# Turning activations through VectorE and a DRAM trip instead of TensorE, in a fused feed-forward, attention, feed-forward kernel

## The chip, the cores and the metric

One core of one Trainium2 chip runs the kernel. The metric is the device time of one execution in microseconds. Three runs of the kernel before give a median of 175.92 us (175.82 to 176.13). "TensorE" (PE in the rows) multiplies, "VectorE" is DVE, "ScalarE" is ACT, "GpSimd" is POOL, and SP is the queue that issues most transfers.

## What is computed

Three residual blocks over x of 4 x 1024 tokens of 128 numbers, in f32:

```
x = x + 0.5 * ffn(layernorm(x))      # first
x = x + attention(layernorm(x))      # linear attention, 16 heads of 8
x = x + 0.5 * ffn(layernorm(x))      # second, same weights

ffn(x):  lt = x[:, 1:17]; even = lt[:, ::2]; odd = lt[:, 1::2]
         m1 = outer(even[:4], odd[:4]) as (512, 128); m2 = outer(even[4:], odd[4:]) as (128, 512)
         h = gelu(x @ (W1 + scale * m1).T + b1);  out = h @ (W2 + scale * m2).T + b2
attn(x): q, k, v = x @ W.T + b;  f(t) = exp(t @ R - 0.5 * |t|^2), t scaled by 1/sqrt(8)
         out = (f(q) @ (f(k).T @ v)) / sum(f(q));  out @ Wo.T + bo
```

W1 and W2 differ for each batch row of x, since `m1` and `m2` come from its own first tokens.

## The kernel before

**Tiles.** Tokens go in chunks of 512 (4 tiles of 128 tokens). There are 16 feed-forward chunks: 0 to 7 in the first part, 8 to 15 in the second, two for each batch row; attention has its own 8. All of x stays in SBUF, in the tile `X`, in three generations.

**A feed-forward chunk f.** VectorE takes statistics (`stats`, L112) and aggregates them (`moments`, L120, L124), GpSimd takes the power -1/2 (L342), VectorE makes the offset (`norm`), ScalarE writes the normalized tile `xn` (L399), tokens on the partitions. The product with W1 needs features on the partitions. Stage `turn` does that: four TensorE transposes of 128x128 into the PSUM bank `ps_t` (L677), ScalarE copies the bank to `xh`, rounded to the short form fp32r (L410), and VectorE subtracts `ps_t - xh` into `xl` (L527). Stage `up.f.j` is three matmuls of 128x512, `xh*w1h + xl*w1h + xh*w1l` (L712 to L714), and a Gelu on ScalarE (L432). Stage `down.f.n` is eight records of 128x128 in f32 (L728); after the fourth, VectorE adds into `X` (L595).

**Weights of a batch row.** `rows.i` sends 16 token rows to DRAM and fetches them back to all partitions as `ev` (L297, L304). `odd` takes the odd tokens from the turned chunk (L535), `w1` adds to W1 (L557), ScalarE rounds (`w1h`), VectorE takes the rest (`w1l`, L568), `w2` adds to W2 (L581). For batch row 0, `w1.0` on VectorE makes all four blocks, rounding included (L562, L564), from rows that TensorE picks out (`select`).

**Attention.** `astats`, `anorm` and `aturn` do for attention's input what `stats`, `norm` and `turn` do: four transposes into `ps_m` (L700), `xah` on ScalarE (L413), `xal` on VectorE (L539). `qk` is three matmuls for each token tile (L745 to L747) into a pair of PSUM banks; `feat` squares on ScalarE (L438), `head_sums` adds per head on VectorE (L604), `feat` subtracts there (L611), `exp` on ScalarE (L446) writes `qk`. Then come `gram` (L763), `z_sums`, `z_eps`, `z` (L617 to L625, and GpSimd's L374), `qturn` (L752), `mix` (L775, L778; VectorE copies its result to `mo`, L635) and `o` (L785, added at L640).

**What sets the order.** Each engine runs its instructions in program order, and the order of stages is written out by hand in the table `ORDER`, one list for each engine. Semaphores carry the dependences. SP works through its list in order as well, and a wait in it holds all that stands behind.

A turn before, on three engines:

```
ins = pe.transpose(ps_t[:, n * P:(n + 1) * P], xn[:, i % XN, n], ident[:])
act.activation(xh[:, i % XT], ps_t[:], ACT.Copy).then_inc(s_hi, 1)
dve.tensor_tensor(xl[:, i % XT], ps_t[:], xh[:, i % XT].bitcast(F32), ALU.subtract)
```

Of the kernel before, what the change touches and what calls it, by code (L numbers as in the profile page):

```python
# [820 lines left out]
```

## Time and profile before

| | us |
|---|---|
| median of three runs | 175.92 |
| the profiled execution's own time | 174.35 |
| its span, first to last instruction | 172.6 |
| TensorE busy | 166.8 |
| VectorE busy | 127.4 |
| ScalarE busy | 123.2 |
| GpSimd busy | 69.4 |

The span is shorter than the execution's time by what lies around the first and last instruction. TensorE's end times are modelled, so its busy time says that it had work in hand, not that it ran at its peak. A group of instructions ("L677 PE MATMUL ...") gives busy time and the mean duration of one; on VectorE and ScalarE an instruction begins before the one ahead of it has fully ended, so the distance between two starts is what one costs.

### The profile page before, as it was taken

What the parts mean: (1) busy time and instruction counts of PE and PEld (TensorE: products, weight loads), DVE (VectorE), ACT (ScalarE), POOL (GpSimd) and SP (SyncE); (2) the same over time, 40 slices, a digit from 0 to 9 for tenths busy, and PEclk for the clock granted to TensorE, in tenths of its full rate; (3) what the DMA queues carried; (4) which work ended last, traced back from release to release, by engine and by line L of the source; (5) the groups of instructions that cost most, each with busy time, mean ns of one, the idle gap of its engine ahead of it and who ended that gap; (6) DMA issues with size and microseconds to landing.
All of it is one profiled execution on the core that took longest, in us unless ns stands there. A gap on an engine that the chain in (4) does not pass through costs nothing.

```text
span 172.6 us, 3454 instructions
## 1 busy us (share of the span) xinstructions
PE 166.8 (97%) x1132; PEld 148.8 (86%) x1132; DVE 127.4 (74%) x446; ACT 123.2 (71%) x241; POOL 69.4 (40%) x85
## 2 busy tenths in 40 slices
PE   6999999999999999999999999899999999999993
PEld 6976998898899989768788898789899989898893
DVE  1888798977967647899999999998957664651111
ACT  3498669598796958779955499986894757557500
POOL 4522196232188089862522544004451399200000
PEclk9999999999999999999999999999999999999999
DMA  4993100404000000000000004310005003521203
GB/s 107 291 281 100 50 0 3 124 4 122 2 0 4 0 2 4 0 0 0 0 0 6 0 4 122 91 36 2 4 8 176 0 0 88 161 90 32 66 13 108
DMA packets 17009, 9.06 MB, mean 53 GB/s; under 512 B 1008, under 2 KB 16608, under 8 KB 16992
## 3 DMA queue, kind: packets, MB, share of 16 engines
q1 hardware_dynamic: 16704, 8.85, 17.4%
q8 instruction: 9, 0.15, 0.4%
q14 instruction: 8, 0.07, 0.1%
q10 hardware_dynamic: 288, 0.00, 0.1%
HBM read 6.69 MB, written 2.15 MB: 51 GB/s over the span
## 4 chain that ended last, share of the span: by engine, by line
PE 90%; DVE 5%; issue 2%; ACT 1%; POOL 0%; POOLq 0%; DVEq 0%; ACTq 0%
PE quad L728 32%; PE quad L712 9%; PE quad L713 9%; PE quad L714 9%; PE ps_t L677 4%; PE quad L745 4%; PE quad L663 4%; PE quad L747 3%; PE quad L746 3%; PE ps_g L763 3%; PE ps_m L700 2%; PE ps_t L785 2%; PE ps_r L752 1%; DVE s L604 1%; PE ps_g L728 1%
## 5 line engine op out<-in xcount | busy, mean ns | idle before, releaser
L728 PEld LDWEIGHTS quad<-w2e,gl 128*128 128x128 f32 x496 | 59.9, 192 | 2.4 <-ACT gl L432 0.2
L728 PE MATMUL quad<-w2e,gl 128*128 128x128 f32 x496 | 60.7, 275 | 0.0
L432 ACT ACTIVATE gl<-quad,cols 128x512 f32<-128x512 f32 x64 | 43.5, 686 | 20.6 <-PE quad L714 20.3
L712 PE MATMUL quad<-xh,w1h 128*128 128x512 f32 x64 | 28.7, 448 | 0.6 <-DVE w1l L568 0.2
L342 POOL TENSOR_TENSOR rstd<-veps,mhalf 128x4 f32<-128x4 f32 (+1 forms) x16 | 16.1, 1011 | 31.3 <-DVE veps L124 29.5
L399 ACT ACTIVATE xn<-X,nmr,rstd 128x128 f32<-128x128 f32 x61 | 24.8, 484 | 3.6 <-DVE nmr L499 3.6
L713 PE MATMUL quad<-xl,w1h 128*128 128x512 f32 x64 | 25.3, 395 | 0.0
L714 PE MATMUL quad<-xh,w1l 128*128 128x512 f32 x64 | 25.2, 394 | 0.0
L595 DVE TENSOR_TENSOR X<-quad,X 128x512 f32<-128x512 f32 (+1 forms) x16 | 10.8, 673 | 15.6 <-PE quad L728 9.9
L363 POOL TENSOR_TENSOR X<-X,b2h 128x512 f32<-128x512 f32 x16 | 20.6, 1311 | 4.1 <-issue 4.1
L374 POOL TENSOR_TENSOR qn<-qk,zr 128x512 f32<-128x512 f32 x8 | 8.6, 1081 | 23.7 <-DVE zr L625 23.6
L112 DVE BATCH_NORM_STATS2 bst<-X 128x6 f32<-128x128 f32 x64 | 13.7, 278 | 4.3 <-DMA X<-in_x_dram 4.2
L712 PEld LDWEIGHTS quad<-xh,w1h 128*128 128x128 f32 x64 | 12.2, 190 | 3.8 <-DVE w1l L564 1.3
L438 ACT ACTIVATE sq<-quad 128x512 f32<-128x512 f32 x16 | 9.5, 595 | 8.1 <-PE quad L747 7.7
L527 DVE TENSOR_TENSOR xl<-ps_t,xh 128x512 fp32r<-128x512 f32 x16 | 10.9, 684 | 5.5 <-ACT xh L410 5.2
L745 PE MATMUL quad<-wah,xah 128*128 128x512 f32 x32 | 14.3, 447 | 0.5 <-DVE ex L611 0.3
L714 PEld LDWEIGHTS quad<-xh,w1l 128*128 128x128 f32 x64 | 12.0, 188 | 2.8
L348 POOL TENSOR_TENSOR arstd<-aveps,mhalf 128x4 f32<-128x4 f32 x8 | 8.1, 1011 | 15.8 <-DVE aveps L124 15.8
L581 DVE SCALAR_TENSOR_TENSOR w2e<-ev,od,w2t 128x128 f32<-128x128 f32 x28 | 11.5, 477 | 3.3 <-DMA ev<-token_rows 3.3
L422 ACT ACTIVATE xa<-X,anmr,arstd 128x128 f32<-128x128 f32 x32 | 13.0, 483 | 0.0
L713 PEld LDWEIGHTS quad<-xl,w1h 128*128 128x128 f32 x64 | 12.2, 191 | 0.8
L747 PE MATMUL quad<-wah,xal 128*128 128x512 f32 x32 | 12.6, 395 | 0.0
(108 smaller groups left out, 279.7 us busy)
## 6 DMA issues: line engine op xcount, KB each, us to landing
ev<-token_rows SPq DMA_DIRECT2D x7, 512.0 KB, 3.7
X<-in_x_dram SPq DMA_DIRECT2D x7, 256.0 KB, 6.4
out_dram<-X SPq DMA_DIRECT2D x7, 256.0 KB, 2.9
w1t<-in_w1t_dram SPq DMA_DIRECT2D x1, 256.0 KB, 3.6
w2n<-in_w2t_dram SPq DMA_DIRECT2D x1, 256.0 KB, 4.7
wa<-in_wa_dram SPq DMA_DIRECT2D x1, 256.0 KB, 6.7
out_dram<-X SPq DMA_DIRECT2D x2, 128.0 KB, 1.8
X<-in_x_dram SPq DMA_DIRECT2D x1, 192.0 KB, 3.3
```

The lines of the kernel that those rows point to most:

```text
L112: ins = dve.bn_stats(bst[:, i, n], x[:, n])
L342: pool.tensor_tensor(rstd[:, i, own], veps[:, i, own], mhalf[:, own], ALU.pow).then_inc(s_rstd, 1)
L363: pool.tensor_tensor(X[:, after], X[:, before], b2h[:].unsqueeze(1).to_broadcast([P, NT, D]), ALU.add).then_inc(s_xb, 1)
L399: act.activation(xn[:, i % XN, n], X[:, xslot(i), n], ACT.Identity, bias=nmr[:, i, n:n + 1], scale=rstd[:, i, n:n + 1]).then_inc(s_xn, 1)
L422: act.activation(xa[:, i, n], X[:, CHUNKS + i, n], ACT.Identity, bias=anmr[:, i, n:n + 1], scale=arstd[:, i, n:n + 1]).then_inc(a_xn, 1)
L432: act.activation(gl[:, f % 2, j], ps_h[j % 2], ACT.Gelu, bias=cols[:, j:j + 1]).then_inc(s_gelu, 1)
L712: pe.matmul(ps_h[j % 2], w1h[:, w, blk], xh[:, f % XT], start=True, stop=False)
L713: pe.matmul(ps_h[j % 2], w1h[:, w, blk], xl[:, f % XT], start=False, stop=False)
L714: pe.matmul(ps_h[j % 2], w1l[:, w, blk], xh[:, f % XT], start=False, stop=True).then_inc(s_u, 1)
L728: ins = pe.matmul(y[:, n * P:(n + 1) * P], gl[:, f % 2, j, n * P:(n + 1) * P], w2e[:, f // PER_B % 2, j], start=(j == 0), stop=(j == HB - 1))
L745: pe.matmul(to, xah[:, a, tile], wah[:], start=True, stop=False)
L747: pe.matmul(to, xal[:, a, tile], wah[:], start=False, stop=True).then_inc(s_qk, 1)
```

## The change

Only chunks 0 to 3 are still turned by TensorE. Chunks 4 to 15 and all eight inputs of attention go another way:

- VectorE's block transpose (`blocks`, `ablocks`) turns each 32x32 block of the normalized chunk in place of its partition quadrant, and writes them to `tq` or `atq` (two slots each) in an order that suits the store.
- SP writes 256 KB to the new DRAM tensor `folded` (`put`, `aput`), waits until it has landed, and reads it back with four transfers of 32 partitions (`land`, `aland`) into `land` (three slots) or `aland` (two).
- ScalarE and the subtraction then read `land` or `aland` in SBUF instead of PSUM. For attention the subtraction goes to GpSimd; `xah` and `xal` shrink from eight slots to five.
- `z_eps` goes from VectorE to GpSimd, the copy to `mo` from VectorE to ScalarE, the rounding of the first W1 blocks from VectorE to ScalarE in four stages `first_w1h`, between VectorE's `first_w1` and `first_w1l`.
- x chunk 3 is loaded before W2, chunks 4 to 7 before `wa` and `rrep`; `w2n` goes, `w2t` is scaled in place. `ps_o` is `ps_t` for all chunks. `ORDER` is new on all five lists.

```diff
+PE_TURNS = (0, 1, 2, 3)
+BY_DRAM = [f for f in range(FC) if f not in PE_TURNS]
+SQ = 32
+LAND, ALAND, TQ, AH = 3, 2, 2, 5
...
+        def folding(t):
+            return t.rearrange("p (b n i) -> p n b i", n=NT, i=SQ)
+        def in_order(t):
+            return t.rearrange("p (q n i) -> p n q i", n=NT, i=SQ)
+        def turned(f):
+            return as_tiles(ps_t[:]) if f in PE_TURNS else in_order(land[:, by_dram(f) % LAND])
+        def as_tiles(t):
+            return t.rearrange("p (n q i) -> p n q i", n=NT, i=SQ)
...
+                if stage == "put":
+                    sp.wait_ge(s_tr, by_dram(i) + 1)
+                    sp.dma_start(folded[i], tq[:, by_dram(i) % TQ]).then_inc(s_put[i], 16)
+                if stage == "land":
+                    sp.wait_ge(s_put[i], 16)
+                    if by_dram(i) >= LAND:
+                        gone = BY_DRAM[by_dram(i) - LAND]
+                        sp.wait_ge(s_lo, gone + 1)
+                        sp.wait_ge(s_od, gone // PER_B + 1)
+                    for b in range(D // SQ):
+                        place = slice(SQ * b, SQ * (b + 1))
+                        sp.dma_start(land[place, by_dram(i) % LAND].rearrange("p (q c) -> p q c", q=P // SQ),
+                                     folded[i].rearrange("(q p) (b c) -> b p q c", p=SQ, c=P)[b]).then_inc(s_land[i], 16)
...
+                if stage == "aturn":
+                    pool.wait_ge(a_hi, i + 1)
+                    pool.tensor_tensor(as_tiles(xal[:, i % AH]), in_order(aland[:, i % ALAND]),
+                                       as_tiles(xah[:, i % AH].bitcast(F32)), ALU.subtract).then_inc(a_lo, 1)
...
-                    act.wait_ge(s_xt, i + 1)
+                    if i in PE_TURNS:
+                        act.wait_ge(s_xt, by_pe(i + 1))
+                    else:
+                        act.wait_ge(s_land[i], 16 * D // SQ)
                     wait(act, s_u, HB * (i - XT + 1))
-                    act.activation(xh[:, i % XT], ps_t[:], ACT.Copy).then_inc(s_hi, 1)
+                    act.activation(as_tiles(xh[:, i % XT]), turned(i), ACT.Copy).then_inc(s_hi, 1)
...
-                    dve.tensor_tensor(xl[:, i % XT], ps_t[:], xh[:, i % XT].bitcast(F32), ALU.subtract).then_inc(s_lo, 1)
+                    dve.tensor_tensor(as_tiles(xl[:, i % XT]), turned(i), as_tiles(xh[:, i % XT].bitcast(F32)),
+                                      ALU.subtract).then_inc(s_lo, 1)
...
+                if stage == "blocks":
+                    dve.wait_ge(s_xn, normed(i, NT - 1))
+                    k = by_dram(i)
+                    if k >= TQ:
+                        dve.wait_ge(s_put[BY_DRAM[k - TQ]], 16)
+                    dve.transpose(folding(tq[:, k % TQ]), as_tiles(flat(xn[:, i % XN]))).then_inc(s_tr, 1)
...
-                if stage == "aturn":
-                    wait(pe, a_lo, i)
...
-                    for n in range(NT):
-                        pe.wait_ge(a_xn, NT * i + n + 1)
-                        ins = pe.transpose(ps_m[:, n * P:(n + 1) * P], xa[:, i, n], ident[:])
-                    ins.then_inc(a_xt, 1)
```

The order at three places. TensorE in attention, around the second chunk's "qk" (`xah` is attention's turned input), before:

```order
L728 MATMUL quad<-w2e,gl 128x128 x8
L700 MATMUL ps_m<-ident,xa 128x128 x4
L728 MATMUL quad<-w2e,gl 128x128 x12
L745 MATMUL quad<-wah,xah 128x512
L746 MATMUL quad<-wal,xah 128x512
L747 MATMUL quad<-wah,xal 128x512
L745 MATMUL quad<-wah,xah 128x512
L746 MATMUL quad<-wal,xah 128x512
L747 MATMUL quad<-wah,xal 128x512
L700 MATMUL ps_m<-ident,xa 128x128 x4
```

and changed:

```order
L822 MATMUL quad<-wal,xah 128x512
L823 MATMUL quad<-wah,xal 128x512
L821 MATMUL quad<-wah,xah 128x512
L822 MATMUL quad<-wal,xah 128x512
L823 MATMUL quad<-wah,xal 128x512
L821 MATMUL quad<-wah,xah 128x512
L822 MATMUL quad<-wal,xah 128x512
L823 MATMUL quad<-wah,xal 128x512
L821 MATMUL quad<-wah,xah 128x512
L822 MATMUL quad<-wal,xah 128x512
```

The transposes `ps_m<-ident,xa` between the "qk" matmuls are gone. VectorE in the middle of attention, before:

```order
L539 TENSOR_TENSOR xal<-ps_m,xah 128x512
L604 TENSOR_REDUCE s<-sq 128x64
L621 TENSOR_SCALAR zs<-zs 128x64
L611 TENSOR_TENSOR ex<-quad,s 128x512
L625 RECIPROCAL zr<-zs 128x64
L604 TENSOR_REDUCE s<-sq 128x64
L539 TENSOR_TENSOR xal<-ps_m,xah 128x512
L611 TENSOR_TENSOR ex<-quad,s 128x512
L617 TENSOR_REDUCE zs<-qk 128x64
L604 TENSOR_REDUCE s<-sq 128x64
L539 TENSOR_TENSOR xal<-ps_m,xah 128x512
```

and changed:

```order
L699 TENSOR_REDUCE s<-sq 128x64
L712 TENSOR_REDUCE zs<-qk 128x64
L706 TENSOR_TENSOR ex<-quad,s 128x512
L626 STREAM_TRANSPOSE atq<-xa 128x4x4x32
L699 TENSOR_REDUCE s<-sq 128x64
L716 RECIPROCAL zr<-zs 128x64
L706 TENSOR_TENSOR ex<-quad,s 128x512
L699 TENSOR_REDUCE s<-sq 128x64
L712 TENSOR_REDUCE zs<-qk 128x64
L706 TENSOR_TENSOR ex<-quad,s 128x512
L626 STREAM_TRANSPOSE atq<-xa 128x4x4x32
```

`xal` and `z_eps` (the TENSOR_SCALAR on `zs`) no longer stand there; `atq<-xa`, a block transpose, does. SP in the second feed-forward part, before:

```order
L304 DMA ev<-token_rows 128x8x128
L297 DMA token_rows<-xn 16x128
L304 DMA ev<-token_rows 128x8x128
L312 DMA out_dram<-X 128x4x128
L297 DMA token_rows<-xn 16x128
L304 DMA ev<-token_rows 128x8x128
L312 DMA out_dram<-X 128x4x128 x6
```

and changed (`folded<-tq` is a put, `land<-folded` a landing in four transfers):

```order
L351 DMA folded<-tq 128x512
L361 DMA land<-folded 32x4x128 x4
L351 DMA folded<-tq 128x512
L361 DMA land<-folded 32x4x128 x4
L351 DMA folded<-tq 128x512
L341 DMA token_rows<-xn 16x128
L348 DMA ev<-token_rows 128x8x128
L351 DMA folded<-tq 128x512
L361 DMA land<-folded 32x4x128 x4
L351 DMA folded<-tq 128x512
L361 DMA land<-folded 32x4x128 x8
L341 DMA token_rows<-xn 16x128
```

Puts and landings now stand between the `rows` steps, and later output stores wait behind them.

## Rows read from the trace of the kernel before

**Rows 1.** The page, part 1: busy time, share of the span, instructions of each engine.
```profile
span 172.6 us, 3454 instructions
...
PE 166.8 (97%) x1132; PEld 148.8 (86%) x1132; DVE 127.4 (74%) x446; ACT 123.2 (71%) x241; POOL 69.4 (40%) x85
```

**Rows 2.** The page, part 2: clock granted to TensorE, 40 slices, tenths of full speed.
```profile
PEclk9999999999999999999999999999999999999999
```

**Rows 3.** The page, part 4: the chain that ended last, by line.
```profile
PE quad L728 32%; PE quad L712 9%; PE quad L713 9%; PE quad L714 9%; PE ps_t L677 4%; PE quad L745 4%; PE quad L663 4%; PE quad L747 3%; PE quad L746 3%; PE ps_g L763 3%; PE ps_m L700 2%; PE ps_t L785 2%; PE ps_r L752 1%; DVE s L604 1%; PE ps_g L728 1%
```

**Rows 4.** The chain in order of time: start us, length us, what.
```profile
11.50 0.48 PE quad L712
...
17.90 1.78 PE quad L728 x16
...
23.93 0.44 PE ps_t L677 x4
...
63.66 0.23 PE quad L745
...
111.09 0.47 PE quad L712
```

**Rows 5.** The same chain where it leaves TensorE, 101 to 110 us; one piece of many.
```profile
103.64 0.86 DVE bst L112 x4
```

**Rows 6.** Stretches: length, busy of PE, PEld, DVE, ACT, POOL, PEclk, DMA share, GB/s.
```profile
65.72:110.14 44.42, 43.59 (x284) 37.32 (x283) 43.32 (x122) 35.72 (x75) 21.56 (x23) 1.00 0.05 13
111.00:170.00 59.00, 58.83 (x420) 53.98 (x420) 33.90 (x113) 37.42 (x68) 17.53 (x15) 1.00 0.21 61
```

**Rows 7.** The timeline of VectorE: start us, us, engine, line, operation, output<-input.
```profile
41.72 1.49 DVE L581 SCALAR_TENSOR_TENSOR w2e<-ev,od,w2t 128x128 f32<-128x128 f32 x4
...
67.04 0.87 DVE L112 BATCH_NORM_STATS2 abst<-X 128x6 f32<-128x128 f32 x4
67.94 0.69 DVE L539 TENSOR_TENSOR xal<-ps_m,xah 128x512 fp32r<-128x512 f32 x1
68.55 0.37 DVE L120 BATCH_NORM_AGGREGATE amv<-abst 128x2 f32<-128x6 f32 x4
...
69.03 0.68 DVE L611 TENSOR_TENSOR ex<-quad,s 128x512 f32<-128x512 f32 x1
...
77.46 0.18 DVE L621 TENSOR_SCALAR zs<-zs 128x64 f32<-128x64 f32 x1
...
107.62 0.28 DVE L635 COPY mo<-ps_m 128x128 f32<-128x128 f32 x1
...
109.46 0.68 DVE L527 TENSOR_TENSOR xl<-ps_t,xh 128x512 fp32r<-128x512 f32 x1
```

**Rows 8.** VectorE and GpSimd side by side; then all passes of w1l (min/median/max ns).
```profile
52.83 2.52 POOL L363 TENSOR_TENSOR X<-X,b2h 128x512 f32<-128x512 f32 x2
...
54.12 2.48 DVE L581 SCALAR_TENSOR_TENSOR w2e<-ev,od,w2t 128x128 f32<-128x128 f32 x4
...
L568 DVE TENSOR_TENSOR w1l<-w1r,w1h x7: 691/693/1174, 21.7 to 152.4; 128x512 fp32r<-128x512 f32 x7
```

**Rows 9.** Groups of instructions, GpSimd: passes over 512 elements.
```profile
L363 POOL TENSOR_TENSOR X<-X,b2h 128x512 f32<-128x512 f32 x16 | 20.6, 1311 | 4.1 <-issue 4.1
...
L374 POOL TENSOR_TENSOR qn<-qk,zr 128x512 f32<-128x512 f32 x8 | 8.6, 1081 | 23.7 <-DVE zr L625 23.6
```

**Rows 10.** DMA issues, KB, us to landing; and the timeline of SP.
```profile
ev<-token_rows SPq DMA_DIRECT2D x7, 512.0 KB, 3.7
X<-in_x_dram SPq DMA_DIRECT2D x7, 256.0 KB, 6.4
out_dram<-X SPq DMA_DIRECT2D x7, 256.0 KB, 2.9
...
142.55 0.32 SPq L297 DMA_DIRECT2D token_rows<-xn  x1
143.91 0.36 SPq L304 DMA_DIRECT2D ev<-token_rows  x1
```

More of the change, by code:

```diff
@@ L216, in build @@
         lead = quad[:, 3]
-        ps_o = [ps_t] * (CHUNKS - 4) + [ps_m] * 3 + [ps_r]
+        ps_o = [ps_t] * CHUNKS
         ld_x = [sem(f"ld_x{c}") for c in range(CHUNKS)]
@@ L233, in build @@
             sem(n) for n in ("r_bst", "r_mv", "r_veps", "r_rstd", "r_nmr", "r_xn", "s_lead")]
+        s_tr = sem("s_tr")
+        s_put = [sem(f"s_put{f}") for f in range(FC)]
+        s_land = [sem(f"s_land{f}") for f in range(FC)]
         s_u, s_gelu, s_d = sem("s_u"), sem("s_gelu"), sem("s_d")
@@ L261, in xslot, with by_dram, by_pe @@
             return f if f < CHUNKS else f + CHUNKS
+        def by_dram(f):
+            return len([k for k in BY_DRAM if k < f])
+        def by_pe(f):
+            return len([k for k in range(f) if k in PE_TURNS])
+        def folding(t):
[6 more added lines that the diff above has]
+            return t.rearrange("p (n q i) -> p n q i", n=NT, i=SQ)
         def normed(f, n):
@@ L304, in _ @@
                     sp.dma_start(ev[:, i % 2], even.partition_broadcast(P)).then_inc(s_ev, 16)
+                if stage == "put":
[11 more added lines that the diff above has]
+                                     folded[i].rearrange("(q p) (b c) -> b p q c", p=SQ, c=P)[b]).then_inc(s_land[i], 16)
+                if stage == "aput":
+                    sp.wait_ge(a_tr, i + 1)
+                    sp.dma_start(folded[FC + i], atq[:, i % TQ]).then_inc(a_put[i], 16)
+                if stage == "aland":
+                    sp.wait_ge(a_put[i], 16)
+                    wait(sp, a_lo, i - ALAND + 1)
+                    for b in range(D // SQ):
+                        place = slice(SQ * b, SQ * (b + 1))
+                        sp.dma_start(aland[place, i % ALAND].rearrange("p (q c) -> p q c", q=P // SQ),
+                                     folded[FC + i].rearrange("(q p) (b c) -> b p q c", p=SQ, c=P)[b]).then_inc(a_land[i], 16)
                 if stage == "down" and i[0] >= CHUNKS and i[1] == NT - 1:
@@ L451, in _ @@
                     act.activation(qt[:, i % QT], ps_r[:], ACT.Copy).then_inc(s_qte, 1)
+                if stage == "mix":
+                    b = i[0]
+                    act.wait_ge(m_mp, b + 1)
+                    wait(act, s_o, PER_B * b)
+                    act.activation(mo[:], ps_m[:, D:2 * D], ACT.Copy).then_inc(m_mo, 1)
                 if stage == "gram" and i % PER_B == PER_B - 1:
@@ L534, in _ @@
                         dve.wait_ge(s_hi, PER_B * i + 1)
-                    dve.tensor_tensor(od[:, i], (lead if i == 0 else ps_t)[:, 2:2 + 4 * LORA:2], scl[:],
+                    dve.tensor_tensor(od[:, i], (lead if i == 0 else ps_t if PER_B * i in PE_TURNS else land[:, by_dram(PER_B * i) % LAND])[:, 2:2 + 4 * LORA:2], scl[:],
                                       ALU.mult).then_inc(s_od, 1)
-                if stage == "aturn":
-                    dve.wait_ge(a_hi, i + 1)
-                    dve.tensor_tensor(xal[:, i], ps_m[:], xah[:, i].bitcast(F32), ALU.subtract).then_inc(a_lo, 1)
@@ new lines, in _ @@
+                    dve.wait_ge(s_ev, 16 * i)
+                    dve.wait_ge(s_w1, LORA * i)
+                    for j in range(LORA):
+                        dve.scalar_tensor_tensor(out=w1r[:, j], in0=ev[:, i % 2, j], scalar=od[:, i, j:j + 1],
+                                                 in1=w1t[:, j * D:(j + 1) * D], op0=ALU.mult,
+                                                 op1=ALU.add).then_inc(s_w1r, 1)
+                if stage == "first w1":
+                    dve.wait_ge(s_od, 1)
+                    dve.wait_ge(ld_w1, 16)
+                    dve.wait_ge(k_sel, min(i + 1, 3))
+                    dve.scalar_tensor_tensor(out=w1r[:, i], in0=picked[i], scalar=od[:, 0, i:i + 1],
+                                             in1=w1t[:, i * D:(i + 1) * D], op0=ALU.mult, op1=ALU.add).then_inc(s_w1r, 1)
@@ L566, in _ @@
+                if stage == "first w1l":
+                    dve.wait_ge(s_w1h, i + 1)
+                    part = slice(D * i, D * (i + 1))
+                    dve.tensor_tensor(w1l[:, 0, part], w1r[:, i], w1h[:, 0, part].bitcast(F32), ALU.subtract).then_inc(s_w1, 1)
                 if stage == "w1l":
```

101 lines of the change are left out of this document (44 added, 57 removed), and 109 rows, old and new, of the table ORDER.

## The prediction

> **What bounds the kernel now.** I read the page's busy table first. TensorE is busy for 166.8 of 172.6 us, VectorE for 127.4, ScalarE for 123.2, GpSimd for 69.4 [rows 1]. The reader is to see that TensorE leaves 5.8 us, while three other engines have a quarter of the span or more. The granted clock is the 2.4 GHz level in every slice [rows 2], so no time is hidden there. The chain of waits says the same by line: TensorE has nearly every entry, and the transposes (`ps_t L677`, `ps_m L700`) have 4% and 2% of the path [rows 3]. The chain in order of time gives prices: four transposes take 0.44 us, sixteen records of "down" 1.78, so a "down" 0.89, a matmul of 512 columns 0.23, so an "up" or a "qk" 0.70, and it marks three places: the first "up" at 11.5 us, the first "qk" near 63.4, `up.8.0` at 111.1 [rows 4]. Between 101 and 110 us the same chain leaves TensorE and runs mostly through VectorE [rows 5]. The stretch view explains it. From 65.72 us (first `head_sums`) to 110.14 (end of `turn.8`) VectorE is busy for 43.32 of 44.42 us; in 111 to 170 us it is busy for only 33.90 of 59.00 [rows 6]. So two engines bound attention together, and TensorE alone bounds the two feed-forward parts.
>
> **1. Transposes leave TensorE.** 12 of 16 stages "turn" and all 8 "aturn" go, four matmuls each. 20 stages x 0.44 us [rows 4] = **8.8 us less TensorE work**. In the feed-forward parts all of it lies on the path. That is the ceiling of the gain.
>
> **2. VectorE turns instead.** 20 instructions of 128x512 are new. No row shows this operation. From below: every pass of VectorE over 512 elements costs 0.60 us from start to start, as `xal` at 67.94 with its follower at 68.55 [rows 7], and none is quicker, so I expect no gain under that. From above: the slowest per element is `w2e`, which writes runs of 32 elements as the new instruction does: four of 128 elements, 512 together, took 1.49 us [rows 7]. I take 0.60, as one instruction of 512 elements is nearest to the passes like `xal`; the upper bound is 0.9 us more for each. The Trainium skill (VectorE: DVE Perf Modes, The three transpose paths) gives 311 ns for a 128x128 bf16 transpose in 32x32 blocks; an estimate from that page is 4 x 0.311 = 1.24 us, which would make the sum about 2.6 us longer in attention. No trace here shows it.
>
> VectorE also gives work away: 8 subtractions of `aturn` (0.61) and 8 `z_eps` to GpSimd, 4 copies `mo` and 4 small casts to ScalarE. An instruction overlaps the one ahead by 0.08 (67.94 + 0.69 against 68.55), so the `z_eps` of 0.18 costs 0.1 and the copy of 0.28 costs 0.2; four statistics take 0.9, a `moments` 0.5 [rows 7]. Between `head_sums.0.0` and `turn.8` the two orders differ by this. Gone: 6 `aturn` 3.7, 2 `down` 1.2, 2 `astats` 1.8, one `amoments` 0.5, 6 `z_eps` 0.7, 3 `mo` 0.6, together 8.5 us. New: 4 block transposes 2.4, `feat.7.1` 0.6, `stats.11` 0.9, `z_sums.6` 0.6, together 4.5. So the stretch needs 4.0 us less: 44.4 becomes 40.4, or 39.3 if the 1.1 us of idle go too.
>
> **3. Attention, where both meet.** TensorE reaches `qk.0.0` later than before: 5 "down" (4.5 us) and `turn.1` stand ahead now, 6 stages of transposes do not; 63.4 + 4.5 + 0.4 - 2.6 = 65.7 us. VectorE then has `down.7.3`, a block transpose and `astats.7` to do, 2.1 us, and starts the heads at 67.8. It ends `turn.8` at 107.1 to 108.2, and `up.8.0` follows 0.95 later as it did (110.14 to 111.09), at 108.1 to 109.2. TensorE alone would be there after 14 transposing stages less (6.2), with `turn.1`, `gram.7` and `mix.3.0` more (1.5): at 111.1 - 4.7 = 106.4. VectorE is later by 1.7 to 2.8 us. I take **2.2 us lost**. After `up.8.0` VectorE keeps up: from there to the end of `turn.9` its order holds 5.6 us at the prices above, TensorE's order 5.9 before `up.9.0`.
>
> **4. Two engines on one path to SBUF.** At 54.12 us one `w2e`, two sources in SBUF, waited for the GpSimd addition beside it (until 55.35): four took 2.48 us instead of the 1.49 of 41.72 [rows 7, 8]. One `w1l` took 1174 ns where the median is 693 [rows 8]. So a two-source pass of VectorE waits for a two-source pass of GpSimd. This change makes more of both: 12 subtractions of `turn` now read `land` and `xh` in SBUF instead of PSUM, and GpSimd gets 8 subtractions of 1.1 to 1.3 us [rows 9]. GpSimd's large passes rise from 24 x 1.31 + 8 x 1.08 = 40 us to 50, 30% of the time; mean wait half a pass. 12 x 0.3 x 0.65 = 2.3 us, nearly all in the feed-forward parts, where VectorE has 40% idle. In attention it meets `turn.8`, `w1.4` and `w1l.4`: **0.3 us**. The Trainium skill (GPSIMD Engine Reference, Specifications) says that GpSimd shares its SBUF interfaces with VectorE, with contention when VectorE has two SBUF inputs; by that rule, and the trace agrees, the 0.3 us stand, with the 1174 ns above; without it this term would be 0.
>
> **5. The DRAM trip.** SP issues one write and four reads for each chunk, in order, and waits for each write before its reads. One issue is 0.36 us. A store of 256 KB lands 2.9 us after issue, `ev` after 3.7 (512 KB) [rows 10]. The last read of 64 KB I take at 2 us, 2.9 at most. So a trip is 2.9 + 4 x 0.36 + 2 = 6.3 us. SP's own turn in the last part is 0.36 + 2.9 + 1.44, half a `rows` step (142.55 to the end of the second issue at 144.27, 1.7 us, so 0.9) and an output store of 0.37: 6.0 us for a chunk, against TensorE's 4 x 0.70 + 4 x 0.89 = 6.4. It fits with 0.4 us to spare and a lead of about two chunks. The tightest first use is chunk 4. Its block transpose stands some 5 us of VectorE's work behind the time of the first "down" (17.9 us [rows 4]), at about 23; written at 23.5, the trip lands near 29.8. ScalarE takes it ahead of the activation of `up.3.0`, which by TensorE's order comes 7 "down", 5 "up" and one turn (10.2 us) after the first "down", at 28.1 to 29. TensorE has three "down" and one "up" (3.4 us) to run before it misses that activation. I cost the trips at **nothing**, covered by those 3.4 us and by the lead.
>
> **6. The small things.** `scale` now stands ahead of the first statistics, `norm.0` ahead of `rest`, and `wa` and `rrep` are loaded last: later by up to 1 us; the casts of W1 on ScalarE and the load of chunk 3 ahead of W2 win about as much. **0, plus or minus 1 us.** GpSimd goes to about 81 us (8 x 1.2 and 8 x 0.2 more) and ScalarE gets 4 copies of 0.3 and 4 casts of about 0.3, both beside TensorE.
>
> **The sum.** -8.8 + 2.2 + 0.3 + 0 = **-6.3 us**. The profiled execution takes 174.35 us around its span of 172.6; it would take 168.0. The three runs have a median of 175.92, 1.6 above that execution, and the figure below is against them: 175.9 - 6.3 = 169.6.
>
> **The rivals.**
> - *TensorE keeps its pace through attention.* For it: VectorE's 1.1 us of idle and some overlap with TensorE's own waits before 111 us. Against: the chain's own path there [rows 5]. Gain 8.8, time 167.1. Chance 0.2.
> - *The transposes cost up to 1.5 us.* The four in the VectorE-bound stretch add 4 x 0.9 = 3.6 us. Time 173.2. For it: the `w2e` row. Chance 0.2.
> - *Slower: SP's queue becomes the bound.* If a write lands after more than 3.3 us, SP's turn passes TensorE's 6.4 us. Loads of 256 KB did take 6.4 us in the crowded start [rows 10]. Then a turn is 9.5 us, 3.1 us too long in 10 chunks (5 to 7 and 9 to 15), less a lead of two chunks in each part (4 x 6.4 = 25.6 us): 5.4 us, nearly all the gain. From a landing of about 6.5 us on the kernel is slower than before; at 7 us the sum is +11.4 and the time 181. Against: from 111 us on the DMA engines are used for 0.21 of the time [rows 6]. Chance 0.09.
> - *It does not do what it says:* the waits between DMA and ScalarE eat just the gain, time about 176. Chance 0.03.
>
> **How the numbers follow.** My case has 0.48. Its own range is 168.5 to 171 (the two ends of part 3 and the start). A measurement of this kernel can tell about 0.2%, or 0.35 us. Faster takes my case and the first two rivals, 0.88; same the last, 0.03; slower the third, 0.09. The range reaches from 166.6 (full gain and half a microsecond of better start) to 174.2 (dear transposes and a start 1 us later); outside lie the two last rivals and little else.
>
> **What would show it.** Right: 80 of TensorE's 1132 matmul records gone, all of them transposes, a `STREAM_TRANSPOSE` near 0.68 us, the `up.8.0` matmul at 108 to 109 us, VectorE still over 95% busy in attention, and ScalarE's `xh` without waits for DMA. Wrong: transposes over 1 us; ScalarE waiting for `land` by more than 1 us in total; SP waiting for `folded` longer than 3.3 us each; `up.8.0` before 107 us; two-source passes on VectorE with a mean over 0.9 us.

## The result and the profile after

The changed kernel takes **170.75 us** (median of 4 runs, 170.62 to 171.91) against 175.87 for the kernel before, run beside it (4 runs, 175.34 to 176.13). The ratio is 0.9751, with an interval of 0.9714 to 0.9788: 4.4 us less (3.7 to 5.0), where 6.3 were forecast. The profiled execution takes 170.79 us around a span of 169.0. That of before was near the fastest that this kernel shows (174.35; on other chips its runs lie between 174.2 and 176.2), so the two traces stand only 3.65 us apart (at TensorE's end), and a few tenths between two traces mean nothing here.

The page of the changed kernel: busy time, granted clock, the chain by engine and by line, DMA issues (KB each, us from issue to landing).

```profile
span 169.0 us, 3429 instructions
...
PE 160.3 (95%) x1052; PEld 141.7 (84%) x1052; DVE 136.8 (81%) x442; ACT 124.3 (74%) x249; POOL 83.5 (49%) x101
...
PEclk9999999999999999999999999999999999999999
...
PE 75%; DVE 8%; ACT 7%; issue 5%; DMA 2%; POOL 1%; DVEq 0%; ACTq 0%; POOLq 0%
...
ev<-token_rows SPq DMA_DIRECT2D x7, 512.0 KB, 4.1
folded<-tq SPq DMA_DIRECT2D x12, 256.0 KB, 2.0
land<-folded SPq DMA_DIRECT2D x48, 64.0 KB, 2.2
```

TensorE has lost 80 of its 1132 instructions [rows 1] and 6.5 us of busy time, yet its idle time has grown from 5.8 to 8.7 us. It has 75% of the chain of waits; VectorE and ScalarE have 8% and 7% (90%, 5% and 1% before). The clock is the 2.4 GHz level throughout, as before [rows 2].

The groups of the new work (instruction, count, busy us, mean ns of one, idle before it):

```profile
L632 DVE STREAM_TRANSPOSE tq<-xn 128x512 f32<-128x512 f32 x12 | 8.3, 701 | 0.8 <-ACT xn L480 0.7
...
L441 POOL TENSOR_TENSOR xal<-aland,xah 128x512 fp32r<-128x512 f32 x8 | 10.2, 1286 | 3.4 <-ACT xah L498 3.4
...
L494 ACT ACTIVATE xh<-land 128x512 fp32r<-128x512 f32 x12 | 7.5, 624 | 2.9 <-DMA land<-folded 2.9
```

A block transpose costs what any pass over 512 elements costs: 0.70 us, 0.63 from start to start (101.72 to 102.35 below). The stretch of attention from the first head sums to the end of `turn.8`, and the last part (the columns are those of [rows 6]):

```profile
68.89:109.15 40.26, 37.24 (x220) 30.80 (x218) 39.10 (x103) 33.58 (x70) 26.55 (x32) 1.00 0.31 93
110.18:166.00 55.82, 55.59 (x391) 50.45 (x389) 39.07 (x109) 37.04 (x67) 16.64 (x15) 1.00 0.38 113
```

To see where the time went I split TensorE's time into work and rest. Work is the number of its instructions times their pitch, 0.232 us for 512 columns and 0.111 for 128 (both from [rows 4]: 0.23, and 1.78 for sixteen), 0.17 for the four of `split_weights`. The rest is waiting, besides the little by which single matmuls start behind their pitch: waits of over 0.12 us each make up 6.5 of the changed kernel's 9.8 us, and 2.6 of the 4.6 before.

| part | before: starts at, length, work, rest | after: starts at, length, work, rest |
|---|---|---|
| `up.0.0` to `up.4.0` | 11.50, 26.42, 25.34, 1.07 | 11.11, 25.70, 23.91, 1.78 |
| to `qk.0.0` | 37.92, 25.49, 25.25, 0.25 | 36.81, 29.75, 28.90, 0.85 |
| to `up.8.0` | 63.41, 47.68, 44.92, 2.76 | 66.56, 43.62, 37.81, 5.81 |
| to TensorE's end | 111.09, 58.67, 58.12, 0.54 | 110.18, 55.92, 54.57, 1.34 |

The work fell by 8.4 us, 76 of the 80 transposes; the time ahead of `up.0.0` has 4 fewer, and there 0.4 us were won. The rest grew by 5.2. Of that growth the 0.6 us ahead of `qk.0.0` are the least certain: six later traces of kernels with the same orders up to there (runs 1, 2, 3, 4 and 8, two for run 1) have a rest of 0.27 to 0.61 in this part, this one 0.85. In the last part the work fell by 3.6 and the length by 2.8; up to `up.8.0` the work fell by 4.9, and only 0.5 us of it is left.

The waits are few and long. TensorE's own rows at four of them, each with its idle time in brackets:

```profile
15.43 0.66 PE L762 MATMUL ps_t<-ident,xn 128*128 128x128 f32 x4 [0.83 <-DVE xl L620]
...
70.43 0.47 PE L821 MATMUL quad<-wah,xah 128*128 128x512 f32 x1 [0.84 <-DVE ex L706]
...
105.75 0.49 PE L851 MATMUL ps_m<-wa,kvm 128*128 128x128 f32 x2 [0.82 <-DVE kvm L720]
...
107.66 1.16 PE L858 MATMUL ps_t<-mo,qt 128*128 128x128 f32 x8 [0.53 <-ACT mo L544]
```

VectorE's timeline ahead of the third, and ScalarE's ahead of the fourth:

```profile
101.72 0.71 DVE L632 STREAM_TRANSPOSE tq<-xn 128x512 f32<-128x512 f32 x1
102.35 0.12 DVE L640 TENSOR_TENSOR od<-land,scl 128x8 f32<-128x8 f32 x1
...
104.05 0.68 DVE L712 TENSOR_REDUCE zs<-qk 128x64 f32<-128x512 f32 x1
104.64 0.86 DVE L120 BATCH_NORM_STATS2 bst<-X 128x6 f32<-128x128 f32 x4
105.42 0.27 DVE L720 TENSOR_TENSOR kvm<-ps_m,bd 128x128 f32<-128x128 f32 x1
```

```profile
105.79 1.65 ACT L480 ACTIVATE xn<-X,nmr,rstd 128x128 f32<-128x128 f32 x4 [0.46 <-DVE nmr L592]
107.35 0.25 ACT L544 ACTIVATE mo<-ps_m 128x128 f32<-128x128 f32 x1
```

A product of 128x128 (`kvm`, 0.27 us) stands behind a head's sum and four statistics, and the copy `mo` (0.25 us) that was given to ScalarE behind a normalization of 1.65. The same copy is behind another wait of 0.53 us at 94.4, and a `qt` copy behind one of 0.50 at 88.4.

### The profile page after: what moved, and what is told of

Same layout as the page of the kernel before. It is cut to its first block, busy times and chain, and to the rows that moved or that the text cites. A ratio compares the mean times of both kernels' runs of the same rounds, so it can differ in the third digit from the quotient of the medians.

```text
span 169.0 us, 3429 instructions
## 1 busy us (share of the span) xinstructions
PE 160.3 (95%) x1052; PEld 141.7 (84%) x1052; DVE 136.8 (81%) x442; ACT 124.3 (74%) x249; POOL 83.5 (49%) x101
## 4 chain that ended last, share of the span: by engine, by line
PE 75%; DVE 8%; ACT 7%; issue 5%; DMA 2%; POOL 1%; DVEq 0%; ACTq 0%; POOLq 0%
PE quad L804 33%; PE quad L788 9%; PE quad L789 8%; PE quad L790 8%; PE quad L821 3%; PE quad L823 3%; PE quad L822 3%; PE ps_t L858 3%; ACT xn L480 3%; PE ps_g L839 2%; DMA scale<-in_rows_dram 2%; ACT gl L520 2%; PE ps_g L804 1%; DVE ex L706 1%; PE ps_r L828 1%
## 5 line engine op out<-in xcount | busy, mean ns | idle before, releaser
L520 ACT ACTIVATE gl<-quad,cols 128x512 f32<-128x512 f32 x64 | 42.6, 682 | 16.6 <-PE quad L790 15.5
L411 POOL TENSOR_TENSOR rstd<-veps,mhalf 128x4 f32<-128x4 f32 (+1 forms) x16 | 16.6, 1043 | 29.1 <-DVE veps L132 29.0
L432 POOL TENSOR_TENSOR X<-X,b2h 128x512 f32<-128x512 f32 x16 | 20.6, 1305 | 1.1 <-issue 1.1
L821 PE MATMUL quad<-wah,xah 128*128 128x512 f32 x32 | 13.6, 426 | 1.0 <-DVE ex L706 0.8
L676 DVE SCALAR_TENSOR_TENSOR w2e<-ev,od,w2t 128x128 f32<-128x128 f32 x28 | 14.2, 568 | 0.0
L620 DVE TENSOR_TENSOR xl<-land,xh 128x512 fp32r<-128x512 f32 x12 | 8.5, 712 | 5.6 <-ACT xh L494 5.6
L822 PE MATMUL quad<-wal,xah 128*128 128x512 f32 x32 | 12.6, 394 | 0.0
```

Source lines behind the costliest of these rows:

```text
L411: pool.tensor_tensor(rstd[:, i, own], veps[:, i, own], mhalf[:, own], ALU.pow).then_inc(s_rstd, 1)
L432: pool.tensor_tensor(X[:, after], X[:, before], b2h[:].unsqueeze(1).to_broadcast([P, NT, D]), ALU.add).then_inc(s_xb, 1)
L520: act.activation(gl[:, f % 2, j], ps_h[j % 2], ACT.Gelu, bias=cols[:, j:j + 1]).then_inc(s_gelu, 1)
L676: dve.scalar_tensor_tensor(out=w2e[:, i % 2, :, out_rows], in0=even[:, j].rearrange("p (o k) -> p k o", k=HB), scalar=od[:, i, LORA + j:LO ...
L821: pe.matmul(to, xah[:, a % AH, tile], wah[:], start=True, stop=False)
L822: pe.matmul(to, xah[:, a % AH, tile], wal[:], start=False, stop=False)
```

## Experiments

The theories of the first four runs: **V**, VectorE sets the pace of attention (step 3 of the prediction); **T**, TensorE's work counts there in full (the first rival); **D**, the DRAM trips hold the chunks up. Each ratio below is to the kernel before, run on the same chip. Against the changed kernel I compare by the quotient with its 0.9751; the intervals are 0.25 to 0.4% wide to each side, so a difference between two kernels is known to about 0.8 us, and the traces must say what smaller ones mean.

**1. More transposes in attention, or behind it**

```diff
                     to = quad[:, n]
+                    if n == 2:
+                        for _ in range(NT):
+                            pe.transpose(to[:, 0:P], ident[:], ident[:])
```

> The changed kernel with four more TensorE transposes ahead of the third qk tile of each of the 8 attention chunks: 8 x 0.44 = 3.5 us more TensorE work inside attention, nothing else. My theory V (VectorE sets the pace of attention, TensorE has about 3 us of room there): at most 1.5 us longer than the changed kernel, 170.8 to 172.3. Rival T (TensorE sets the pace everywhere and the missing gain went elsewhere): 3.0 to 3.5 us longer, about 174.

> The changed kernel with four more TensorE transposes at 8 places of the second feed-forward part (ahead of up.9.0 to up.15.0 and down.15.0): 3.5 us more TensorE work there. Theory V, which says that TensorE alone bounds this part: 3.0 to 3.5 us longer, about 174. Rival D (the DRAM trips or the shared path to SBUF hold TensorE up in this part): under 2 us longer.

Measured: 173.53 us, ratio 0.9922 (0.989 to 0.9954), 3.0 us more than the changed kernel, for 3.5 us of work in attention. The same work in the last part (a stage of four transposes ahead of eight of its "up" and "down"): 174.08 us, 0.9954 (0.9918 to 0.999), 3.6 us more. V, as far as it says that TensorE has room in attention, falls; T has the size right. TensorE's instructions fall behind the changed kernel's steadily: they are 0.46 us ahead of them at `qk.0.0` and behind by 1.52 at `qk.5.0`, 1.97 at `qk.6.0`, 2.34 at `qk.7.0` and 2.41 at `up.8.0`.

**2. Reads that don't wait for the write**

```diff
-                    sp.wait_ge(s_put[i], 16)
...
-                    sp.wait_ge(a_put[i], 16)
```

The reads take x instead of `folded`, in the same shapes.

> The landings read rows of the input x instead of folded and no longer wait for the write; writes, reads, their number and their sizes stay, what is computed is not what was asked. It takes the waiting on the write out of every trip (about 2 us each). Theory V: the trips are covered, so between 0.5 us shorter and 0.3 us longer than the changed kernel. Rival D (ScalarE waits for landings and hands the wait on): 2 us shorter or more.

Measured: 171.07 us, 0.9767 (0.9727 to 0.9806), not shorter. D falls for the waits on the writes. It doesn't fall for what stands in SP's queue between write and read; that is run 7.

**3. Shorter block transposes**

```diff
-                    dve.transpose(folding(tq[:, k % TQ]), as_tiles(flat(xn[:, i % XN]))).then_inc(s_tr, 1)
+                    m = NT if k < TQ else 1
+                    dve.transpose(folding(tq[:, k % TQ])[:, 0:m], as_tiles(flat(xn[:, i % XN]))[:, 0:m]).then_inc(s_tr, 1)
```

The same for `atq`. Three of four tiles of these chunks are left out.

> 16 of the 20 block transposes turn only one of the four tiles (a quarter of the elements; the rest of the slot keeps older data), so VectorE saves about 16 x 0.4 = 6.4 us, 4 x 0.4 = 1.6 of it inside the attention stretch. Theory V: 1.3 to 2 us shorter than the changed kernel, all of it ahead of up.8.0. Rival T: within 0.4 us of it.

Measured: 170.13 us, 0.9712 (0.9688 to 0.9737), 0.7 us less, between the two forecasts and not clear of noise, for 7.4 us less of VectorE's busy time (129.4 against 136.8). The stretch is not shorter (its row stands with the others below): VectorE's load fell by 1.2 us in it, and its idle time rose by as much. So work taken from VectorE alone gives next to nothing in attention, and work given to TensorE alone costs nearly all. After this the theory was **M**: attention isn't bound by VectorE's load; the waits in chains across engines bound it.

**4. Stages moved, nothing added: the waits for `kvm`, `mo` and `qt`**

```diff
 TensorE
-gram.4 mix.1.1 ... qk.7.3 mix.2.0
+mix.1.1 gram.4 ... mix.2.0 qk.7.3
 ScalarE
-feat.4.1 qturn.1 ... aturn.7 feat.5.1 qturn.2 mix.1.1 ... norm.10 mix.2.1
+qturn.1 feat.4.1 ... qturn.2 aturn.7 feat.5.1 mix.1.1 ... mix.2.1 norm.10
 VectorE
-z_sums.6 stats.11 mix.2.0
+mix.2.0 z_sums.6 stats.11
```

> The changed kernel with eight stages moved in three orders, nothing added or left out. TensorE: mix.1.1 ahead of gram.4, mix.2.0 ahead of qk.7.3. ScalarE: the copies qt of chunks 1 and 2 ahead of the second squares of chunks 4 and 5, the mo copy of mix.2.1 ahead of norm.10. VectorE: mix.2.0 ahead of z_sums.6 and stats.11. Theory M (attention isn't bound by VectorE's load; TensorE waits there in chains that pass over other engines, above all for the mo copy that the change gave to ScalarE): the waits at 88.4 (0.50), 94.4 (0.53), 104.7 (0.98) and 106.9 us (0.70), 2.7 us in sum, go; 1.9 to 2.7 us less than the changed kernel, about 168.3 us, ratio to the kernel before about 0.960, and the stretch from the first head sums to the end of turn.8 shrinks from 40.3 to about 38. Theory V (VectorE, 39.1 us busy in those 40.3, sets the pace): the stretch can't fall below 39.1, so at most 1.1 us less, and likeliest under 0.5.

Measured: 171.68 us, 0.9797 (0.9762 to 0.9831): 0.8 us **more**, at the edge of the noise and in any case not the 1.9 to 2.7 less of M. The waits for `qt` at 88.4 and for `mo` at 106.9 went, that for `kvm` at 104.7 too, that at 94.4 became two of 0.47 and 0.32, and three new ones came, over TensorE's pitch: 1.12 us at 103.1 for `gs`, 0.89 at 107.3 for `qn` and 1.34 at 108.7 for the exponentials of chunk 7. TensorE's row at the first, then ScalarE's and SP's timelines:

```profile
104.42 0.49 PE L804 MATMUL ps_m<-gs,wv 128*128 128x128 f32 x2 [0.95 <-ACT gs L505]
```

```profile
102.04 0.63 ACT L450 ACTIVATE xh<-land 128x512 fp32r<-128x512 f32 x1 [1.00 <-DMA land<-folded]
102.58 1.14 ACT L490 ACTIVATE qk<-ex 128x512 f32<-128x512 f32 x2
103.62 0.57 ACT L495 ACTIVATE qt<-ps_r 128x512 f32<-128x512 f32 x1
104.10 0.27 ACT L505 ACTIVATE gs<-ps_g 128x128 f32<-128x128 f32 x1
```

```profile
93.35 0.34 SPq L307 DMA_DIRECT2D folded<-tq  x1
93.73 1.92 SPq L297 DMA_DIRECT2D token_rows<-xn  x1
96.91 0.38 SPq L304 DMA_DIRECT2D ev<-token_rows  x1
97.40 1.94 SPq L317 DMA_DIRECT2D land<-folded  x4
```

The engines came 0.6 us earlier to the same place, and chunk 8 had not landed: its reads stand in SP's queue behind a round trip of `token_rows` and the 512 KB of `ev`. In this trace it landed at 102.0, 2.7 us after SP had issued the last of them. In the changed kernel that was issued by 98.6 and landed at 100.9, 0.7 us ahead of ScalarE's 101.6; in run 2 ScalarE waited for it too, for 1.28 us. Some of this is chance of the one trace: chunk 8's write landed after 3.4 us here and after 2.0 in the changed kernel, and the 16x128 write behind it took 1.92 us to issue instead of 0.43. But the queue is enough by itself: in the trace of run 5, with the same order there, both were as usual, and ScalarE waited 0.87 us.

**5. The same, and the start**

```diff
 VectorE
-moments.3 moments.4 turn.1
+turn.1 moments.3 moments.4
```

> The same moves, and at the start one more: on VectorE xl of chunk 1 ahead of the two moments stages of chunks 3 and 4, which hold it up by 0.7 us while TensorE waits 0.99 us for it at 14.2 us. Theory M (each wait of TensorE counts in full): 0.6 to 0.7 us less than with the attention moves alone, about 167.7 us, qk.0.0 0.6 us earlier. Rival (the start's wait is given back before attention, since VectorE's moments are then 0.7 us later and norms, and with them later turns, too): the same time as with the attention moves alone, within 0.2 us.

Measured: 171.71 us, 0.9815 (0.9777 to 0.9853), no gain. `turn.2` came 0.7 us earlier, and then `up.1.0` waited for the Gelu of chunk 0: it starts at 16.19, in the changed kernel at 16.23, and `up.4.0` starts at 36.78 and 36.81. The rival was right, one step sooner than I had it.

**6. The kernel before with 57 transposes fewer**

```diff
-                    for n in range(NT):
+                    for n in range(NT) if i < 4 else (NT - 1,):
...
-                    for n in range(NT):
+                    for n in range(NT) if i < 1 else (NT - 1,):
```

> The kernel before with one of the four TensorE transposes in the turns of chunks 4 to 15 and in attention's turns 1 to 7 (the others are left out, so the turned inputs hold old values): 57 transposes fewer at 0.109 us, 6.2 us off TensorE, and nothing added anywhere. Theory M (TensorE's work counts nearly in full in the kernel before too): 5.3 to 6.2 us less, about 169.2 us, ratio about 0.966. Theory V (attention is VectorE's, 43.3 of 44.4 us busy before): the transposes left out inside attention, about 33 of the 57 or 3.6 us, gain at most 1.1; 3.0 to 3.7 us less, about 172 us, ratio about 0.980.

Measured: 173.04 us, 0.9878 (0.9833 to 0.9924): 2.1 us less, for 6.3 us of work. That is less than either theory gave, so M falls too where it lets TensorE's work count nearly in full. TensorE's rest rises from 4.6 to 9.4 us, also in the last part (0.54 to 2.21), where I had seen only TensorE at work: the longest two waits there are 0.38 us idle ahead of a turn for ScalarE's `xn` and 0.23 for VectorE's `xl`.

**7. Chunk 8 read ahead of `ev`; then, besides, statistics moved back**

```diff
 SP
-put.8 rows.4 (write, wait, ev) land.8
+put.8 rows.4 (write) land.8 even.4 (wait, ev)
 VectorE, in the second run only
-z_sums.6 stats.11 norm.10 ... o.4 moments.11
+z_sums.6 norm.10 ... o.4 stats.11 moments.11
```

> The kernel with the mix stages and qt copies moved earlier, and on SP's queue one more move: the four reads of chunk 8's trip (land.8) go ahead of the 512 KB read of the even rows (ev of rows.4), behind which and the wait for token_rows they stood. Theory Q (that kernel lost its gain because ScalarE then waits 1.00 us at 101.0 us for chunk 8 to land, 6.9 us after the transpose instead of the usual 4.2, and the exponentials and gs queue behind it, so TensorE waits 1.12 us for gs): the reads issue 1.5 to 2.1 us earlier, ScalarE's and TensorE's waits there go, and with them the two later ones (0.89 and 1.34 us) shrink; 1.5 to 2.5 us less than with the mix moves alone, about 169.7 us, ratio to the kernel before about 0.968, stretch about 39.5. Rival (VectorE's 39.3 us and the chains between engines hold the stretch at 40.2 to 41.8 however the trip goes; another wait takes its place): within 0.5 us of the mix moves alone, ratio about 0.977 to 0.980.

> The same, and on VectorE the four sums of stats.11 (0.87 us) behind z.6 and o.4 instead of ahead of chunk 7's head sums. Theory M (what ends the stretch is the chain sq, head sums, ex, exp, gram of chunk 7, and each VectorE instruction queued ahead of it counts): up.8.0 0.6 to 0.9 us earlier, 0.5 to 0.9 us less than without this move. Rival (VectorE's sum sets the time, and the order of the same work doesn't matter): within 0.2 us.

Measured: 170.85 us, 0.9764 (0.9727 to 0.9801), and with stats.11 late 170.61 us, 0.974 (0.9711 to 0.977). ScalarE's and TensorE's waits for chunk 8 went, the stretch fell from 41.78 to 40.67 and to 39.91, and `up.8.0` came at 110.49 and 109.76. Against run 4 that is 0.6 us (within the noise) and 1.0 us of time. Under half of what Q expected; and the sum only leads back to the changed kernel, from which neither can be told apart. In the first of the two, waits of 0.87 and 1.34 us stayed, for `qn` and for chunk 7's exponentials; in the second the one for `qn` went and the other is 1.49.

**8. More work on VectorE in attention**

```diff
+                    if p == 1:
+                        dve.reciprocal(spare[:, a % 3], wa[:, 0, 0:NT * HEADS])
```

> The changed kernel with one reciprocal of 128x64 added on VectorE behind the second ex of each of the 8 attention chunks, 8 at 0.46 us start to start, 3.7 us, its result unused. Theory I (interlock: VectorE and TensorE both have fixed orders and two buffers between them, so work added to either counts nearly in full and work taken from one alone gives little): 2.5 to 3.7 us more than the changed kernel, about 173.8 us, ratio about 0.992 to 0.996. Theory L (what is left of the stretch are latencies between engines, and VectorE has room in them, as the transposes made short suggested): under 1.5 us more.

Measured: 174.15 us, 0.9934 (0.9905 to 0.9963), 3.2 us more. The total is in I's range and outside L's. The trace doesn't put all of it on the added work. TensorE is 0.14 us behind the changed kernel at `qk.0.0` and 0.20 at `qk.5.0`, after four additions; 0.95 at `qk.6.0` after five, 1.43 at `qk.7.0` after six, and then 4.04 at `up.8.0`. The last 2.6 us came with two events. Chunk 8's write landed after 4.0 us instead of 2.0; ScalarE waited 1.77 us for the chunk, and TensorE 0.78 for `gs` and 1.40 for `kvm` behind it (nothing and 0.98 in the changed kernel). And `w1l.4` took 1.76 us instead of 0.72, beside an addition of GpSimd, while TensorE waited for it ahead of `up.8.0`. ScalarE's row, then VectorE's, GpSimd's and TensorE's:

```profile
104.38 0.63 ACT L495 ACTIVATE xh<-land 128x512 fp32r<-128x512 f32 x1 [1.77 <-DMA land<-folded]
```

```profile
112.20 1.76 DVE L664 TENSOR_TENSOR w1l<-w1r,w1h 128x512 fp32r<-128x512 f32 x1
```

```profile
111.66 1.76 POOL L433 TENSOR_TENSOR X<-X,b2h 128x512 f32<-128x512 f32 x1
```

```profile
114.22 0.47 PE L791 MATMUL quad<-xh,w1h 128*128 128x512 f32 x1 [1.05 <-DVE w1l L664]
```

So **work added to TensorE in attention costs nearly all of itself (run 1), and work removed from one engine alone gives a third of itself or less (runs 3 and 6)**. That work added to VectorE does the same holds for the total only: the first six additions, 2.8 us, cost TensorE 1.3, and whether the two events belong to the added work or to chance is not shown. The same stretch in seven kernels, with VectorE's column the fourth (DVE); in order: run 1, run 8, run 3, run 6, run 4, then the two of run 7.

```profile
68.42:111.57 43.15, 40.49 (x249) 33.87 (x248) 39.50 (x103) 33.54 (x70) 26.71 (x32) 1.00 0.29 87
```

```profile
69.03:112.29 43.26, 38.41 (x222) 31.20 (x221) 41.88 (x111) 33.69 (x71) 27.00 (x33) 1.00 0.31 91
```

```profile
68.30:108.52 40.22, 37.27 (x220) 30.82 (x218) 37.89 (x102) 33.55 (x70) 26.58 (x32) 1.00 0.31 93
```

```profile
65.64:109.37 43.73, 42.04 (x264) 35.01 (x262) 42.95 (x122) 35.71 (x75) 21.82 (x23) 1.00 0.05 13
```

```profile
68.29:110.07 41.78, 37.59 (x220) 30.48 (x218) 39.29 (x103) 33.62 (x71) 26.58 (x32) 1.00 0.31 91
```

```profile
68.80:109.47 40.67, 37.45 (x220) 30.51 (x218) 39.16 (x103) 33.51 (x71) 26.58 (x32) 1.00 0.30 93
```

```profile
68.68:108.59 39.91, 37.40 (x220) 30.50 (x218) 38.44 (x99) 33.06 (x70) 26.58 (x32) 1.00 0.31 94
```

VectorE's busy time bounds the stretch from below, though not rigidly (the 3.7 us added in run 8 raised it by 2.8), and in six kernels (before, changed, run 8, run 6 and the two of run 7) the stretch lies 0.8 to 1.5 us above it. It lies 2.3 to 3.7 us above it where VectorE was made lighter (run 3), TensorE heavier (run 1) or a landing late (run 4). In run 9 it is 1.7.

**9. GpSimd's additions with one source**

```diff
-                    pool.tensor_tensor(X[:, after], X[:, before], b2h[:].unsqueeze(1).to_broadcast([P, NT, D]),
-                                       ALU.add).then_inc(s_xb, 1)
+                    pool.tensor_scalar(flat(X[:, after]), flat(X[:, before]), 0.0, None, ALU.add).then_inc(s_xb, 1)
```

The same for attention's eight passes; b2 and bo are left out.

> The changed kernel with GpSimd's 24 passes over X (bias of the 16 chunks, and of attention's 8 inputs) as a plain copy plus 0.0 with one source; the additions of b2 and bo are left out. Theory C (the 12 VectorE instructions that are stretched 0.4 to 1.2 us beside GpSimd's two-source passes, 9.8 us in sum against 3.2 before, are what ate the gain): 1.5 us or more less, ratio below 0.967, and none of the 12 is stretched. Rival (nearly all of the 9.8 us lie where VectorE is ahead, outside attention's stretch): the stretched ones go, and the time is 0.2 to 0.7 us less.

Measured: 172.02 us, 0.9817 (0.9779 to 0.9854), 1.2 us more. The excess of held-up VectorE instructions over their medians fell from 9.8 to 4.4 us, still in twelve cases, and a GpSimd pass of this form takes longer:

```profile
L432 POOL TENSOR_SCALAR X<-X 128x512 f32<-128x512 f32 x16 | 24.5, 1542 | 1.2 <-issue 1.2
```

that is 1542 ns where the addition took 1305. So the run doesn't isolate the collisions. It only shows that 5.4 us less of them didn't make the kernel shorter; what they cost stays open here. The trace of the changed kernel bounds what they cost directly: none of the twelve lies in attention's stretch; from 16.3 to 36.8 us TensorE has no wait over 0.12 us, and its rest grew by 0.6 us from there to `qk.0.0` and by 0.8 behind `up.8.0`.

**10. The end of attention, relieved on both engines**

```diff
 GpSimd
-aturn.7 z.5
+aturn.7 turn.8 w1l.4 z.5
 VectorE
-turn.8 w1l.4 z.6
+z.6
 ScalarE
-feat.7.0 feat.7.1 mix.2.1 norm.10 w1h.4
+feat.7.0 w1h.4 feat.7.1 mix.2.1 norm.10
 TensorE
-gram.6 o.4 qturn.5 gram.7 up.8.0 mix.3.0 o.5 up.8.1
+gram.6 o.4 up.8.0 up.8.1 qturn.5 gram.7 mix.3.0 o.5
```

On VectorE `o.3`, `norm.10` and the first `feat.7.0` move forward besides.

> The kernel with the mix moves, the reads of chunk 8 first and stats.11 late, and at the end of attention 1.2 us of VectorE's work given to GpSimd, which is idle for 4.3 us there: xl of chunk 8 (at 102 us) and w1l of block 4 (at 105 us, with ScalarE's w1h ahead of the last squares); TensorE runs up.8.0 and up.8.1 ahead of the transposes of qn and of gram.7, in its wait of 1.49 us at 107.3 us for the last exponentials; VectorE's nmr and od of that place are moved out of the way of GpSimd's passes, and its last ex of the first half goes ahead of the second head sums. Theory I (interlock: only work taken from both engines together at the same place shortens it): TensorE's wait there goes, up.9.0 comes 1.2 to 1.5 us earlier; 1.2 to 1.6 us less than without this edit, about 169.2 us, ratio to the kernel before 0.965 to 0.967. Rival (collision: GpSimd's two added passes of 1.3 us hold up VectorE's small instructions and qn, and the gain is given back; or another wait takes its place): within 0.4 us, ratio 0.972 to 0.976.

Measured: 170.92 us, 0.9754 (0.973 to 0.9777), the time of the changed kernel. `up.8.0` came at 107.30, 2.5 us earlier than with stats.11 late; `up.9.0` came at 116.32, 0.3 us later (this trace is 0.5 us later at `up.0.0` but only 0.1 at `qk.0.0`). TensorE's rows between them:

```profile
107.30 0.47 PE L745 MATMUL quad<-xh,w1h 128*128 128x512 f32 x1
...
110.77 0.49 PE L805 MATMUL ps_m<-gs,wv 128*128 128x128 f32 x2 [0.37 <-ACT gs L506]
...
113.35 0.49 PE L808 MATMUL ps_m<-wa,kvm 128*128 128x128 f32 x2 [0.76 <-DVE kvm L677]
```

The work brought forward was only taken from the place where it had covered the last chain (`gram.7`, `gs`, `kvm`, `mo`), which ends when it ended before. The rival held: another wait took its place.

## Why the prediction was right, and where it was not

**Direction and range** held: faster, 170.75 in 166.6 to 174.2, and at the far end of my own case's 168.5 to 171. The gain was 6.3 by forecast and 4.4 by the ratio. Of the signs, the 80 transposes, 0.70 us for each new one and VectorE at 97% of attention's stretch were seen. Two failed: `up.8.0` came at 110.2, not 108 to 109, and ScalarE waited 2.9 us in total for `land`, where over 1 us was to mean that the forecast is wrong. One slip in the rivals: for the slow SP queue "the sum is +11.4" is that rival's loss; with the 6.3 gained the sum is +5.1, which is the 181 that stands beside it.

**Step 1, the ceiling.** Right: 8.4 us of work gone after `up.0.0`, 0.4 ahead of it. But "in the feed-forward parts all of it lies on the path" was too strong: run 6 took 6.3 us of it from the kernel before and got 2.1. In the changed kernel the last part gave 2.8 of 3.6; there the orders of the other engines were new as well, and which of the two matters was not tested.

**Step 2, block transposes.** The lower bound was the value: 0.63 us from start to start, 0.60 taken. The dear rival (1.49), and the 1.24 of an estimate from the Trainium skill (VectorE: DVE Perf Modes, The three transpose paths), don't hold for this type and shape; the stretch was to take 40.4 us and took 40.26.

**Step 3, attention.** The size was right and the sentence behind it half right. "TensorE alone would be there at 106.4, VectorE later by 1.7 to 2.8" reads as if TensorE had 2.2 us of room there. Run 1 showed none: 3.5 us more on TensorE cost 3.0. Run 3 showed that VectorE's relief alone gives 0.7 us for 7.4. Run 8 is less clear on VectorE's own room: 2.8 us more on it cost TensorE 1.3 up to `qk.7.0`, and the rest of its 3.2 came with a late landing and a collision. The two engines stand in fixed orders with two buffers between them; whichever is late is waited for by the other. `up.8.0` came at 110.2 where 108.1 to 109.2 was forecast, because the stretch began 1.1 us late (68.9, not 67.8): the time up to `qk.0.0` brought 1.3 us of new waits that no step had (0.7 ahead of `up.4.0`, and the 0.6 that other traces show smaller).

**Step 6, the start.** Its 0 hid them: `turn.2` waits 0.99 us at 14.2 for an `xl` that now stands behind two `moments`. Run 5 shows that this alone isn't the price, as ScalarE is as late there.

**Step 4, collisions.** The mechanism was right, its place was not. I priced the twelve subtractions: they take 712 ns where those from PSUM take 685, 0.3 us in all. The collisions meet others too: five of `w2e`, two `nmr`, one `od`, one of the subtractions, and three one-source instructions. GpSimd's timeline, then VectorE's:

```profile
59.59 1.28 POOL L437 TENSOR_TENSOR X<-X,rows 128x512 f32<-128x512 f32 x1
```

```profile
59.70 1.20 DVE L132 TENSOR_SCALAR aveps<-amv 128x4 f32<-128x4 f32 x1
```

Twelve such cases hold 9.8 us over their medians (170 ns for this one), against six and 3.2 before. The Trainium skill (GPSIMD Engine Reference, Specifications) names contention for VectorE's instructions with two SBUF inputs and for those in a 2-port performance mode. Most of the twelve have two inputs, and for them the trace agrees. This row has one; whether it ran in such a mode, no run here shows. None of the twelve lies in attention's stretch, where 0.3 us were charged, so their price there was 0 in this trace. Run 8 shows that it need not be: its `w1l.4`, which step 4 names, was held by 1.0 us, and TensorE with it.

**Step 5, the DRAM trip.** Mostly cheaper than taken: 2.0 us for the write (median) where 2.9 was taken, 2.2 for a read. Two of the twelve writes landed after more than the SP rival's 3.3 (4.6 us at 127.0 and 3.5 at 129.7), too few to fill the queue: SP's longest wait for a write is 1.6. "I cost the trips at nothing" held in this trace, though not as forecast: ScalarE waits for landings four times, 2.9 us in sum, at 42.3, 119.6, 132.7 and 138.3, and within 3 us behind them TensorE has no wait over 0.2. But it missed a place that the order shows: the reads of chunk 8 behind `rows.4`. Run 4 hit it as soon as the engines were 0.6 us faster.

**The sum.** Forecast -8.8 + 2.2 + 0.3 + 0. In the traces: -8.4 of work and -0.4 ahead of `up.0.0`, + 5.2 of new waits: 1.3 in the first half, 3.1 in attention, 0.8 in the last part. The step that was off in size is the one that charged 2.2 us for attention and nothing elsewhere; in its place stand 5.2 us on the traces, so that 3.65 us of gain remain (4.4 by the ratio). No run takes the change apart, so how much of the gain is owed to the transposes alone and how much to the work that VectorE gave away with them is not shown. Run 6 says only that 57 of the 80 transposes, taken off the kernel before with nothing else changed, gave 2.1 us.
